# A fused two-layer decoder kernel: four passes per turn of its loop in place of two

## The reference

```
for each batch element:                      # S = 256 rows, D = 256, 16 heads
  # layer 0
  x += attention with rope, 16 heads of 16, low-rank K and V   (stream "m")
  x += cross attention over the head axis, 16 heads of 64      (stream "h")
  x += gated FFN on the top half of the rows by router score   (stream "h")
  # layer 1
  x += attention, of each row of scores only the 25 largest kept
       (all others 0 before the softmax)                       (stream "t")
  x += attention over ctx, keys beyond a length masked         (stream "c")
  x += linear layer with a ternary weight, plus bias           (stream "c")
```

## Time and profile before

| | |
|---|---|
| median of 3 runs | 6144.0 us (6123.77 to 6145.41) |
| profiled execution | 6155.05 us |
| its span in the profile | 6153.3 us |
| blocks "start" and "first", to the clear behind them | 394.5 us |
| loop: 14 turns, 28 passes | 5181.4 us |
| block "last" | 576.8 us |
| PE busy | 5445.3 us, 88% of the span |
| DVE / ACT / POOL busy | 4576.2 / 3707.2 / 2164.3 us |

### The profile page before, as it was taken

One profiled execution on the slowest core, in us unless ns is written; L12 is line 12 of the kernel. 1 busy time (PEld: TensorE's weight loads), 2 busy tenths in 40 slices (PEclk: granted clock), 3 DMA queues, 4 the chain that ended last, 5 costly groups with the idle time before them and its releaser, 6 DMA issues. The chain is left out here.

```text
span 6153.3 us, 112087 instructions
## 1 busy us (share of the span) xinstructions
PE 5445.3 (88%) x39324; PEld 3838.9 (62%) x39324; DVE 4576.2 (74%) x16189; ACT 3707.2 (60%) x9249; POOL 2164.3 (35%) x3076
## 2 busy tenths in 40 slices
PE   7899899888898989898888898989889898898987
PEld 4666566666666666566666666666666666666654
DVE  2477787677887777787777887777887787887784
ACT  3466566665676656666665666656666565666642
POOL 0233433333343333343333443333433233433331
PEclk7799999999999999999999999999999999998976
DMA  2000000000000000000000000000000000000000
GB/s 86 4 6 5 8 8 6 7 8 7 6 6 10 5 7 6 8 8 6 7 8 7 6 6 10 5 7 6 6 10 6 7 5 10 6 6 6 5 4 6
DMA packets 29383, 53.47 MB, mean 9 GB/s; under 512 B 8145, under 2 KB 9810, under 8 KB 27986
## 3 DMA queue, kind: packets, MB, share of 16 engines
q1 hardware_dynamic: 28770, 45.73, 2.4%
HBM read 37.33 MB, written 8.39 MB: 7 GB/s over the span
## 5 line engine op out<-in xcount | busy, mean ns | idle before, releaser
L1032 DVE MATCH_REPLACE8 wk<-m,wk 128x256 f32<-128x256 f32 x2048 | 823.4, 410 | 0.0
L1053 POOL TENSOR_SCALAR mx<-m 128x2 f32<-128x2 f32 x512 | 121.6, 238 | 1918.0 <-DVE wk L1032 1917.9
L1028 DVE MAX8 m<-wk 128x8 f32<-128x256 f32 x2048 | 760.7, 414 | 0.0
L467 DVE TENSOR_REDUCE m_nm<-bankM 128x2 f32<-128x512 f32 x1024 | 652.5, 684 | 126.2 <-PE bankM L457 124.8
L798 ACT ACTIVATE xk_area<-bankH,xb 64x256 f32<-64x256 f32 x1024 | 480.4, 469 | 397.4 <-PE bankH L700 380.1
L1062 POOL TENSOR_TENSOR t_pr<-t_pr,sc 128x512 f32<-128x512 f32 x512 | 651.9, 1273 | 40.2
L1060 POOL TENSOR_TENSOR t_pr<-wk,sc 128x512 f32<-128x512 f32 x512 | 658.9, 1287 | 2.1 <-PE bankT L558 0.9
L989 ACT ACTIVATE t_pr<-t_pr,t_nm 128x256 f32<-128x256 f32 x1024 | 465.0, 507 | 192.0 <-POOL t_pr L1062 191.5
L516 PE MATMUL bankM<-m_q,m_kT 32*128 32x512 f32 x2048 | 572.8, 639 | 0.0
L457 PE MATMUL bankM<-m_kT,m_q 32*128 32x256 f32 x4096 | 546.2, 400 | 8.1 <-DVE m_nm L467 5.7
L558 PE MATMUL bankT<-ident,t_pr 128*128 128x128 f32 x2048 | 350.2, 297 | 115.7 <-ACT t_pr L989 112.9
(11 more groups left out here) (223 smaller groups left out, 11916.4 us busy)
## 6 DMA issues: line engine op xcount, KB each, us to landing
xin<-x_in SPq DMA_DIRECT2D x32, 256.0 KB, 2.6
ctxA<-ctx_in SPq DMA_DIRECT2D x32, 256.0 KB, 2.6
ctxB<-ctx_in SPq DMA_DIRECT2D x32, 256.0 KB, 3.0
out<-x SPq DMA_DIRECT2D x32, 256.0 KB, 2.0
w<-w_w SPq DMA_DIRECT2D x2, 1024.0 KB
xwq<-w_xwq SPq DMA_DIRECT2D x1, 1024.0 KB
xwk<-w_xwk SPq DMA_DIRECT2D x1, 1024.0 KB
xwv<-w_xwv SPq DMA_DIRECT2D x1, 1024.0 KB
```

The source lines that it names most:

```text
L467: nc.vector.tensor_reduce(b["nm"][:, i % 2, 2 * (i // 2) + x, :], banks[u % 4][:].rearrange("p (j s) -> p j s", j=2), AX.X, ALU.max, negat ...
L1028: link.inc(nc.vector.max(top, src[:, t, :]))
L1032: m = nc.vector.match_replace(out=wk[:, k, t, :], in_to_replace=take, in_values=src[:, t, :], imm_value=-BIG)
```

## The change

LAPS goes from 2 to 4: the body of the loop holds four passes, and the loop takes 7 turns in place of 14. Elements, passes (28 in the loop) and the blocks "start", "first" and "last" are as before: (32 - 3) // 4 is 7 turns, which leaves 4 elements for "last", as (32 - 3) // 2 = 14 turns did. The order tables of the loop are written anew for four passes on each engine (the letters of each stream are those of two passes doubled), and FILL has four strings for each stream. Of the tables PE's is shown; those of the other engines are cut.

```diff
 
 ORDER = {
     "pe": runs("""
-        c h3 c t2 h c t c t c h c2 t c h t h c h2 c h t h c h c h t h t c t c h2 c h c t c h c2 h t c t c t h c2 h t h c2 m h c h c2 h2 t c
-        h t c t c h3 c t m h2 t h t2 c h2 m c m2 t h m2 t h m h t m h t m h m h2 m t m h m t m t m t m5 t m c m h t m h t m3 t m h m2 h t m
-        h t m t m h4 t h4 t h2 t c h2 c t h t c t c2 m t c h2 c2 h t h2 c2 h t h2 c h t h c t h c t h c h c t c h t c h c2 t c h t c2 h2 c2
-        t h2 c3 t h2 c t h c t h2 c t h c h2 t h m t c t c h2 m2 t m h m2 h2 t m t m h2 m t m h2 m2 t h t m t m t m2 t m4 h m2 t m t h m3 t
-        m h m2 h c t m h t m t m h5 t h3 t2 h2"""),
+        h3 c t c t h c t c t c h c2 t c h t h2 c h c h t h c h c h t h t c t c h2 c h c t c h c2 h t c t c t h c2 m h t h c2 h c h c2 h2 t c
+        h t c t c h3 c t m h2 t h t2 c h2 m c m2 t h m2 t h2 m t m2 t h2 m h m t h m h m t m t m t m4 t m3 c h t m h t m3 t m2 h m h t m h t
+        m t m h4 t h4 t h c t h3 c t h t c t c2 t m c h2 c2 h t h2 c2 h t h2 c h t h c t h c t h c2 h t c h t c h c2 t c h t c2 h2 c2 t h2
+        c3 t h2 c t h c t h2 c t h c h2 t h m t c t c h2 m2 t m h m2 h2 t m t m h2 m t m h2 m2 t h t m t m t m2 t m3 h m3 t m t h m3 t m h
+        m2 h t m h t m t m h4 t h4 t h c h t h2 c t h c t c t c h c2 t c h t h c h2 c h t h c h c h t h t c t c h2 c h c t c h c h c t c t c
+        t h c2 h t h c2 h c2 h c m h2 t c h t c t c h2 c t m h3 t h t2 c h2 m c m2 t h m2 t h m h t m h t m h m h m h t m h m t m t m t m5 t
+        c m2 h t m h t m3 t m h m2 h t m h t m t m h4 t h4 t h c h3 c t2 h t c t c2 m t c2 h2 c h2 t h c2 h t h2 c h t h c t h c t h c h c t
+        c h t c h c2 t c h c t c h2 c2 t h c3 t h3 c t h c t h c h t h c h2 t h m t c t c h2 m2 t m h m2 h2 m t m h t h m t m h2 m2 t h t m
+        t m t m2 t m4 h m2 t m t h m3 t m h m2 h t m h t m t m h5 c h t h2 t h t h"""),
     "act": runs("""
...
     "dve": runs("""
...
     "pool": runs("""
...
-LAPS = 2
-
-FILL = {"t": ["00020100", "02000011"],
-        "h": ["10011000100", "10001001000"],
-        "c": ["02", "12"],
-        "m": ["110", "010"]}
+LAPS = 4
+
+FILL = {"t": ["00020100", "02010111", "00020101", "02010011"],
+        "h": ["20111000100", "00211000000", "00121000100", "01111100000"],
+        "c": ["00", "12", "21", "12"],
+        "m": ["110", "010", "110", "010"]}
 FILL_FIRST = {"t": ["02221000"],
         "h": ["21122000220", "22221000002"],
         "m": ["020", "100"]}
```

More of the change, by code:

```diff
@@ L108 @@
-        m h m2 h c t m h t m t m h5 t h3 t2 h2"""),
-    "act": runs("""
[L110 to L115, removed]
@@ L116 @@
-    "dve": runs("""
[L117 to L120, removed]
+        h3 c t c t h c t c t c h c2 t c h t h2 c h c h t h c h c h t h t c t c h2 c h c t c h c2 h t c t c t h c2 m h t h c2 h c h c2 h2 t c
@@ new lines @@
+    "act": runs("""
+        h2 c h t c h c h t h c t2 h t2 c h t5 h t h2 t h3 m t h2 t2 h t h2 t h t h2 t c2 h2 c t2 h2 t c2 h t h t2 c h2 t c2 t h2 t h2 c t c2
+        h t h3 t c3 h4 t c h t h2 c t h3 c t c h t c h2 t h3 t h t c t h4 t h t3 h m t h2 t h3 t c h t h t h3 m4 t4 h2 t2 h t h t h t h2 t4
+        m t m t m2 t m2 t m t c m2 t4 m2 t h m3 h t3 m2 t m2 h t h t m t h t m h t h2 c h c t h t h t c t3 h t3 c h t h t h7 t3 h2 t2 h3 t2
+        h t h2 c t h2 t c2 h t h c2 t h2 t c t c t m t h2 t c h4 t c3 h4 t2 c3 h2 t h2 c t3 h t c h5 c2 h t c h t h4 t3 h c h5 t4 h t h m h
+        t h c h3 t m t2 h m h m t m t h3 t2 h t2 h3 t3 h2 t5 m t m t m t2 m4 t2 m2 t2 m2 t h m3 t h t2 m2 t m h m t h m t2 h t m h t h c h2
+        t h c h2 c t h t c t4 h c h t4 h t h2 t h3 t h t h3 t m t h t h t h2 t c2 h t h t h2 c t c2 t h t c h t h2 t c2 t h2 t h2 c t c t c
+        h4 t c3 h4 t2 c h c h2 t h3 c t c h t c h t h4 t c h t2 h4 t h t3 h m t h2 t h3 t c t h2 t h2 m4 t3 h t h2 t h t h t h t h t h t4 m
+        t m2 t c m2 t m2 t2 m2 t4 m2 h t m3 h t3 m2 t m2 t h2 t m t h t m h t h2 t h c h2 t h c t c t2 h t2 c h t3 h t h6 t3 h t h4 t3 h t h
+        c t h3 c2 t h t h c2 t h2 t3 c m c t h2 t c h4 t c3 h4 t c t c2 h2 t h2 c t4 c h6 c2 h t c h t h4 t h t2 c h5 t4 h t h m t c h4 t h
+        t2 m h2 m2 t m t h t h3 t h t2 h2 t h t h t6 m t m t2 m t m4 t2 m2 t2 m2 t h m3 h t3 m h m t m t m h m t2 h t m h t h2 t c"""),
@@ new lines @@
+    "dve": runs("""
+        c2 t h c h t c t2 c h2 t c4 m c2 t4 c t c t2 c2 t c3 t c3 t2 m t8 m t2 h t3 h2 t h t h t h t4 h2 t c3 m h t h t h t c t c h c t c t2
+        h2 t4 c t2 m2 h m2 h m2 t m4 t m3 t m2 t m t4 h t2 h2 t2 h t5 h t2 c h6 m h2 m2 t2 m t2 h3 c t c t2 c h c t2 h c3 m c t c2 t2 c3 t c
+        t4 c6 t13 m h t2 h2 m t h2 t4 h2 t3 h m h t c3 t h t2 c h c h c t c h t4 c h t3 h t m3 t m2 h m3 t m4 t m2 t m t2 m t3 h t h2 t2 h
+        t7 h t h6 m2 h m t m h t3 h c2 t h c t2 h2 c t c h t c3 m c3 t c t3 c t2 c t c t c3 t c3 t7 m t3 h m t5 h2 t h t2 h2 t3 h t h t c3 h
+        m t h t h c t c t h c t c h t2 h t4 c t h2 m2 t m4 t m4 t m5 t m t6 h t h2 t3 h t5 h t h6 c m3 t h m t3 c h2 c2 h t2 h t c h t h t
+        c3 m c t c2 t2 c2 t c t c t3 c6 t12 h m t2 h2 t m t h t2 h t2 h2 t3 h m h t c3 t h2 t2 c2 h c t c t2 h t2 h t c t2 h t m4 t m4 h t
+        m4 t m t2 m3 t3 h t2 h t h t h t7 h t h6 m3 h t3 m h t h2 t c"""),
@@ L121 @@
     "pool": runs("""
-        c3 t4 h4 t4 m t2 c t10 h2 t5 h t m2 t h t h t2 c3 t2 h t3 h t h t3 c m t4 h t h t2 m t6 h2 c t c t3 h2 t6 c t3 h t3 h t5 m t m t2 h2
-        t h t3 c2 t h c2 h t5 h t h t5 m t3 h2 t3 h t6 h t"""),
-}
-LAPS = 2
-FILL = {"t": ["00020100", "02000011"],
-        "h": ["10011000100", "10001001000"],
-        "c": ["02", "12"],
-        "m": ["110", "010"]}
+        c2 t h t2 c h2 t h t6 c t2 m t9 h2 t m t2 m h t h t3 h c t c t2 c t2 h t2 h t h t4 m t3 h c h t3 m t6 h2 t c2 t3 h2 t3 h t3 c t6 h
@@ new lines @@
+        t5 m t h t h m t3 h t2 h c2 t h c t7 h2 t4 m t3 h2 t2 c t h t6 c t2 h t m t h c h t3 h t3 c t9 h t3 h m h t3 m t2 h t c t c t h t2 h
+        c t4 h2 t2 m t2 c t3 h2 m t9 h c2 t2 h t h t h t6 c t2 h t7 h t2 m t h t3 m h t h t2 c3 t2 h t4 h2 t h t5 m t3 h2 t3 h t5 c h t2"""),
+}
+LAPS = 4
[3 more added lines that the diff above has]
+        "m": ["110", "010", "110", "010"]}
```

## The result

The changed kernel takes 6103.5 us (median of 8 runs, 6076.3 to 6110.3) against 6142.4 of the kernel before (8 runs, 6123.8 to 6158.8). The ratio is 0.9914, with a 95% interval of 0.9896 to 0.9933: 53 us less, 41 to 64. The two medians alone lie 39 us apart. I had forecast 56 less and 6088. Of all runs in this document one, of o_dve (6198.8 us), fell in a slower state of the chip with a lower clock; it is left out of that kernel's ratio. The profiled execution took 6107.7 us, its span is 6105.9, the loop 5136.9 of it, which was 5181.5.

What follows compares the result with a forecast made beforehand. TensorE was taken to bound the kernel, stalling at each jump back. From the profiled 6155.05 us, 59.5 less for seven jumps and meetings plus 4 for fillers gave 6099.5, or 6088 for the median; range 6050 to 6122.

Steps and rivals of the forecast that it cites:

- What bounds the kernel: In the loop: TensorE (PE), busy 88% of the span, with a 5.63 us wait at each of 13 jumps back.
- The price of jump and meeting: At the loop's jump back: each one removed saves 8.5 us (8.2 to 8.8), seven save 59.5 us.
- The reading of the 53 GB/s: DMA traffic in the gap at the jump, against 4 at the inner seam, taken to agree with an instruction fetch stall.
- The order tables at nothing: New step orders on all engines: small shifts costed at nothing, possibly wrong by about 1 us a pass either way.
- The bound of 28 us: Error allowed for small order shifts: about 1 us a pass, the spread between second passes, over all 28 passes.
- The seam: New middle of the turn: `h:v0` covers L907, so PE does not idle; a failed cover would cost 6 us.
- The fillers at +4: 63 added filler matmuls in the loop: taken as +4 us, with ends of +16 and -42.
- The signs: New profile: six L700 waits near 34 us, branch still 3.6 us, seam without idle, passes without a jump 180 to 182.5 us.
- the fillers win clock: Rival: fillers added in passes 1 to 3 raise the clock, 2 us for each of 21 passes, about 6045; chance 0.14.
- the seam give the gain back: Rival: PE idles at the new middle seam, 6148, or 6118 with half; part of a case with chance 0.14.
- the branch cheap: Rival: the jump is cheap and its idle gap returns wherever a new pass starts, 6148; chance 0.02.
- The slower case: Rival: moved fillers lose the clock, 3.9 us in each of 28 passes, 109 us, giving 6197; chance 0.06.

Runs made afterwards that it cites:

- o_dve: Old tables and fillers of two passes written out twice (four passes a turn), but VectorE's table is the new one: 6150.0 us, ratio 0.9994 to the kernel before.
- e2: Kernel before with two blocks of two passes per turn, old tables and fillers: all 14 meetings, seven jumps; 6086.0 us, ratio 0.9917.
- e5: Kernel before with its loop written out as 14 blocks: all 14 meetings, no jump, old tables and fillers; 6030.0 us, ratio 0.9822.
- e1: Four passes per turn, but the old order tables and old fillers of the kernel before written out twice; 6072.3 us, ratio 0.9894.
- o_dve_pool: Old tables and fillers written out twice, but VectorE's and GpSimd's tables are the new ones: 6166.6 us, ratio 1.0034 to the kernel before.
- e7: Kernel before as one block of 28 passes, old tables 14 times over, no jump and no meeting inside; 6003.0 us, ratio 0.9764.
- e8: e7 with 14 fillers in each pass directly ahead of TensorE's wait for the row selection; 6018.5 us, ratio 0.9788 to the kernel before.

## Why the prediction was right

- **What bounds the kernel** was right: PE, with the jump as the one place where it idles once a turn. e2 and e5 show it.
- **The price of jump and meeting**: 8.5 us for each, seven times, 59.5 us in all. The row of turn 1 gave the jump alone well: 8.2 us, against 181.6 us passes in e2, as forecast, and 8.4 us a jump in e5 by the ratio. The reading of the 53 GB/s as instruction fetch was wrong in its number; they are the load of ctxB. For jump and meeting together e1 gives 65 us by the ratio and 78 in the profiled loops: between the passes 189.9 - 178.8 = 11 us each, above my upper end of 8.8. I had taken the mean of the second passes, 180.92, for a first-pass order with a soft seam; the first-pass order is 2 us shorter there.
- **The order tables at nothing** was the term that failed. With the old fillers they cost 22 to 28 us; with the new ones the measures lie between nothing and 41. My count of exchanged pairs said rightly that the new turn is nearly the old one twice, and wrongly that this makes it equal: DVE's table alone, with 27 to 38 of its pairs in each pass the other way round, costs 61 us, by waits for DVE's results behind which PE runs at half clock. I had argued from DVE's idle time of 40 us in a pass, but what counts is when each result comes. The bound of 28 us that I had given for all passes is about what the order cost.
- **The seam** was right: no idle time where `h:v1` stands ahead of `c:KV`.
- **The fillers at +4** are neither shown nor refuted: the medians say +5 and +7, the ratios -16 and +14, the profiled loops +12 and -7.
- **The signs**: six waits of L700 for 33.9 us, the branch at 3.65 us and the seam came as forecast. The passes did not: I had 187 to 191.7 us behind a jump and 180 to 182.5 for all others, and found 190.3 to 194.4, and 177.6 to 186.6. The third passes are past the 183 us at which I had said that the argument fails. What fails there is the order at nothing, not the price of the jump: the same seam with the old tables has 178.8 us (e1).
- The sum came out near in part by luck, because two errors met: the seam was worth more than I said (65 to 78 in place of 59.5), and the order cost what I had left out. The change as a whole is the unrolling less 12 us by the ratios (65 against 53, with overlapping intervals), and 31 by the medians of two groups.
- **The rivals**: that the fillers win clock did not come, nor did the seam give the gain back, nor is the branch cheap; the Trainium skill's rule ("Runtime: NRT & Kernel Launch", instruction fetch mechanics), by which a taken branch stalls for the fetch of its target when that lies outside the pages held at the time, agrees with e2 and e5. The slower case named the right path, a moved step that loses the clock, but fillers for its cause; DVE's and POOL's order did it, and o_dve_pool is the kernel in which it came, slower than before by 0.3%.

## What to carry to other kernels

A hardware loop around a long body has its price at the jump back, in this kernel about 8 us on the bounding engine (5.6 us idle, then matmuls at half clock), while a meeting of all engines with a clearing of semaphores costs 3 us or less. So write out as many turns as the program may hold, and do it with the order that is already good: with the old tables written out 14 times the kernel takes 6003 us, 2.4% below before and 1.5% below the change by the ratios.

An order table of one engine can't be judged by itself. PE's and ACT's new tables did nothing beside old ones, DVE's cost 61 us there, and all four together cost 28. Look for results of another engine that the bounding engine waits for, even when that other engine is idle for a fifth of the time.

Price a pass by a pass that the trace already has without the thing to be removed. The 181.6 us of turn 1 came back to 0.1 us in e2, and 107 and 141 us were forecast for e5 and e7 where 109 and 145 came by the ratios. Where I took a pass of another order for it (180.9 us), it was 2 us off.

Work added to hold the clock in one place can lose it in another, so add up every pass: e8 gained 37 us in its second passes and lost 25 in its first.

## What the runs showed of the hardware

A taken jump stalls PE alone among the branches (3586 and 3650 ns in the median, DVE's 72), but DVE's first work behind it comes only after 4.1 us of idle time.

A clock of 0.50 once entered can hold for 23.9 us with PE busy 92% of the time (22.07 of 23.90), where the spell behind the jump into turn 2 is over within 6 us of work (0.50 from 761.0 to 764.0, 0.78 to 767.0, then 1.00); no run here tells why. Idle time of PE alone does not say whether the clock falls: it fell behind 1.52 us in o_dve and held through 1.77 us in e2.

Low clock costs less than its length, and about the same in two places: 9.6 us for 23.9 us of it in o_dve, 2.4 us for 6.8 us behind the row selection in e7's second pass, which is 0.40 and 0.35 us for each us.
